# Reordered masking, logarithms and copies in a fused attention and feed-forward kernel, with a third buffer of exponentials

## The reference, cut to what matters

```python
qkv = x @ w_qkv.T; q, k, v = split_heads(qkv); k_y = split_heads(x @ w_ky.T)
L, L_y = q @ k.T / 4, q @ k_y.T / 4
agg = sum(exp(clip(L_y, -15, 15)) * mask, keys) + 1e-6
r = log(abs(L) + 1e-6) - log(agg + 1e-6)
w = softplus(r) * mask
attn = ((w / (sum(w) + 1e-6)) @ v) @ w_proj.T
x = layernorm(x + attn)
h = silu(x @ w1.T * s1) * (x @ w2.T * s2)
h = gelu(h @ h1.T * s_h1); h = gelu(h @ h2.T * s_h2)     # 1024 wide
out = layernorm(x + h @ w3.T * s3)
```

## Time and profile before

| | us |
|---|---|
| median of 3 runs | 1240.26 |
| the profiled execution's own time | 1239.5 |
| its span | 1237.8 |
| PE busy | 1184.8 (96%) |
| DVE busy | 714.9 (58%) |
| ACT busy | 659.0 (53%) |
| POOL busy | 205.5 (17%) |
| first matmul of the feed-forward | at 561.79 |

### The profile page before, as it was taken

One profiled execution on the slowest core, in us unless ns is written; L12 is line 12 of the kernel. 1 busy time (PEld: TensorE's weight loads), 2 busy tenths in 40 slices (PEclk: granted clock), 3 DMA queues, 4 the chain that ended last, 5 costly groups with the idle time before them and its releaser, 6 DMA issues.

```text
span 1237.8 us, 23984 instructions
## 1 busy us (share of the span) xinstructions
PE 1184.8 (96%) x8222; PEld 805.6 (65%) x8222; DVE 714.9 (58%) x1178; ACT 659.0 (53%) x1004; POOL 205.5 (17%) x238
## 2 busy tenths in 40 slices
PE   6899999999999999879999999999999999999997
PEld 2444444544444444437888888888888888888886
DVE  3577778787878787875345435344344353443444
ACT  4688989899888888755114133232242332322421
POOL 2434333434333333300000000000000000000000
PEclk7999999999999999989999999999999999999999
DMA  5555758576776765277000100001000001000010
GB/s 150 120 141 136 215 158 223 156 228 166 216 191 186 204 169 144 56 234 268 34 34 1 36 16 17 34 0 34 17 0 34 17 17 34 0 34 17 0 34 18
DMA packets 62544, 117.28 MB, mean 95 GB/s; under 512 B 8992, under 2 KB 14624, under 8 KB 62496
## 3 DMA queue, kind: packets, MB, share of 16 engines
q1 hardware_dynamic: 62064, 116.12, 32.9%
q10 hardware_dynamic: 432, 0.52, 0.2%
HBM read 46.35 MB, written 19.92 MB: 54 GB/s over the span
## 4 chain that ended last, share of the span: by engine, by line
PE 80%; DVE 9%; issue 5%; ACT 4%; DMA 1%; DVEq 0%; POOL 0%; ACTq 0%; POOLq 0%; SPq 0%
PE score_banks L1360 53%; PE acc_bank L1272 8%; PE score_banks L1244 6%; DVE w_ring L904 4%; PE misc_bank L1236 3%; PE misc_bank L1199 3%; PE misc_bank L1340 2%; ACT w_ring L656 2%; ACT e_ring L649 1%; PE misc_bank L1303 1%; DVE base_v L957 1%; DVE e_ring L895 1%; PE misc_bank L1207 1%; PE misc_bank L1319 1%; DVE e_ring L889 1%
## 5 line engine op out<-in xcount | busy, mean ns | idle before, releaser
L728 ACT ACTIVATE f_h_full<-score_banks,f_scales 128x512 f32<-128x512 f32 x128 | 87.5, 689 | 340.8 <-PE score_banks L1360 340.7
L904 DVE TENSOR_TENSOR w_ring<-score_banks,keep 128x1024 int32<-128x1024 int32 (+1 forms) x192 | 194.0, 1040 | 28.1 <-PE score_banks L1244 27.3
L1360 PE MATMUL score_banks<-f_ha_hi,f_w_all 128*128 128x512 f32 x512 | 204.0, 399 | 0.0
L1360 PE MATMUL score_banks<-f_hb_hi,f_w_all 128*128 128x512 f32 x512 | 203.6, 398 | 0.0
L1360 PE MATMUL score_banks<-f_hb_lo,f_w_all 128*128 128x512 f32 x512 | 201.6, 394 | 0.0
L1360 PE MATMUL score_banks<-f_ha_lo,f_w_all 128*128 128x512 f32 x512 | 200.8, 392 | 0.0
L656 ACT ACTIVATE w_ring<-w_ring 128x1024 f32<-128x1024 f32 (+1 forms) x192 | 172.5, 918 | 24.3 <-DVE w_ring L904 24.2
L649 ACT ACTIVATE e_ring<-score_banks 128x1024 f32<-128x1024 f32 (+1 forms) x192 | 158.3, 877 | 39.4 <-PE score_banks L1244 36.0
L513 POOL TENSOR_SCALAR_AFFINE_SELECT e_ring<-e_ring 128x512 f32<-128x512 f32 (+1 forms) x96 | 80.4, 837 | 285.8 <-DVE e_ring L895 145.0
L1082 DVE CAST f_ha_hi<-f_h_full 128x512 fp32r<-128x512 f32 x64 | 27.3, 426 | 160.5 <-ACT f_h_full L728 160.5
L1360 PEld LDWEIGHTS score_banks<-f_ha_hi,f_w_all 128*128 128x128 f32 x512 | 96.1, 188 | 24.6
(11 more groups left out here) (143 smaller groups left out, 1759.1 us busy)
## 6 DMA issues: line engine op xcount, KB each, us to landing
piece<-in_wf SPq DMA_DIRECT2D x44, 256.0 KB, 2.9
wf_copy<-piece SPq DMA_DIRECT2D x44, 256.0 KB, 3.0
ky_stack<-ky_hi SPq DMA_DIRECT2D x64, 128.0 KB, 2.4
ky_stack<-ky_lo SPq DMA_DIRECT2D x64, 128.0 KB, 2.4
k_stack<-k_hi SPq DMA_DIRECT2D x64, 128.0 KB, 2.6
k_stack<-k_lo SPq DMA_DIRECT2D x64, 128.0 KB, 2.6
f_w_all<-wf_copy SPq DMA_DIRECT2D x2, 4096.0 KB, 24.6
f_x_turn<-x SPq DMA_DIRECT2D x9, 512.0 KB, 3.2
```

Of the source, the lines that this page charges most:

```text
L728: nc.scalar.activation(h_full[m % 2][:], f_bank[m % F_RING], ACT.Gelu, scale=scales[:, 1 + layer, m:m + 1]).then_inc(gelu_done, 1)
L904: nc.vector.tensor_tensor(w_ring[:, t % RING, 2 * i:2 * i + 2, 0:cols].bitcast(I32), pair_banks(place(t, i), cols).bitcast(I32), keep[:, a ...
L1360: mm = nc.tensor.matmul(out, left.bitcast(dt), right.bitcast(dt), start=first and n == 0, stop=last and n == 1)
```

## The change

Nine things are changed, all in the order of the work or in a buffer count:

1. `FIRST_PAIR`: in beats 1 and 2 of a slot DVE does `absolute` of pair 0, then the clip, then `absolute` of pair 1. Before it did the clip first.
2. The check piece of the fifth beat (t = 4) goes to the sixth (t = 5), to a place behind the copies there. `add_differences` goes from the end of beat 1 on DVE to its start, ahead of `keep_agg`.
3. The second `turn` of a finished batch (t = 3) goes behind `sum_weights` on PE, and `turn_keep` behind `copy_sums` on ACT.
4. `E_RING` is 3 (the zone for it is 10 KB larger).
5. `STACK_WARM`: five matmuls of 2x512 on ones, whose result nobody reads, ahead of the first scores.
6. In `beginning`, `scores_y(k, 3)` stands ahead of `ky_proj`, and `scores_y(k, 4)` ahead of `q_proj`.
7. `ending` has a new order on PE, ACT and DVE.
8. The last `sum_weights` of the ending goes into the feed-forward, behind its first tile (m = 0), and `project_out(6, 1)` behind the second. Its `residual` follows on DVE after the third.
9. `residual(6, 0)` goes behind `f_turn_lo` on DVE.

The diff, cut to its core (the ending's lists are shown as rows below):

```diff
-E_RING = 2
+E_RING = 3
+STACK_WARM = 5
-CHECK_BEATS = (0, 2, 3, 4)
+CHECK_BEATS = (0, 2, 3, 5)
+FIRST_PAIR = (1, 2)
...  scalar, slot
-                    if check_step(t, check) is not None:
+                    if t < 5 and check_step(t, check) is not None:
                         check_piece(k, check_step(t, check))
...
+                    if t == 5 and check_step(t, check) is not None:
+                        check_piece(k, check_step(t, check))
-                    if t in (2, 3) and output is not None:
-                        turn_keep(output, t - 2)
+                    if t == 2 and output is not None:
+                        turn_keep(output, 0)
                     if t == 4:
                         k_keep(k)
...
                     if t == CHUNKS:
                         copy_sums(k, 0, (True, 0 in w))
+                    if t == 3 and output is not None:
+                        turn_keep(output, 1)
...  vector, slot
+                    if t == 1 and check_step(0, check) is not None:
+                        add_differences(k.index - FIRST_CHECK - 1)
                     if t == 1 and before[0]:
                         keep_agg(k.shift(-1), 1)
                         factors(k.shift(-1))
...
+                    elif t in w and t in FIRST_PAIR:
+                        absolute(k, t, (0,))
+                        clip(k, t)
+                        absolute(k, t, (1,))
...
-                    if t == 1 and check_step(0, check) is not None:
-                        add_differences(k.index - FIRST_CHECK - 1)
...  tensor, attention_tail and slot
+                if (layer, m) == ("gated", 0):
+                    sum_weights(Unit(BATCH, 1), 2, True)
+                if (layer, m) == ("gated", 1):
+                    project_out(BATCH - 2, 1)
...
                     if sums[1]:
                         sum_weights(*last, not sums[0])
+                    if t == 3 and output is not None:
+                        turn(output, 1)
...  tensor, beginning
+                scores_y(k, 3, y_pair_alone, 1)
                 ky_proj(k1)
-                scores_y(k, 3, y_pair_alone, 1)
                 sum_exps(k, 1, True)
+                scores_y(k, 4, y_pair_alone, 1)
                 q_proj(k1)
                 sum_exps(k, 2, True)
-                scores_y(k, 4, y_pair_alone, 1)
...  tensor, before the run
+            for _ in range(STACK_WARM):
+                nc.tensor.matmul(score[0:2, 2 * BANK_PAIRS - 1, :], ones[:], acc_copy[:], start=True, stop=True)
```

## The result

The changed kernel takes 1244.99 us (median of 18 runs, 1237.76 to 1249.8) against 1239.86 for the kernel before (18 runs, 1237.6 to 1243.02). The ratio is 1.0043, with a 95% interval of 1.0029 to 1.0056: it is slower by 0.43%. The forecast was 1238.6 us, a gain of 0.9 us and too small to tell. So its direction was wrong. The measured time lies just inside the stated range, by 0.01 us at its upper end. The profiled execution took 1243.9 us, with a span of 1242.2 (before: 1239.5 and 1237.8).

The account below looks back on a forecast made before the run. PE bounds the feed-forward from 562 us on; before that it loses little in the loop, more at both attention ends. Terms 0.5 + 0.6 + 0.9 - 1.1 = 0.9 us gained from 1239.5: 1238.6 us, 8-in-10 range 1233.0 to 1245.0.

Parts of the forecast that it names:

- The second turn: Loop, six even slots: the turn's 0.69 us wait mostly moves ahead of the flip; 0.5 us gained, bounds 0 and 4.1.
- Rival A: Loop: the turn's 0.69 us stay won, as the flip needs only `copy_sums` early; 1234.0 us, chance 0.24.
- First pairs ahead of the clip: Loop, beats 1 and 2: beat 3's scores wait less, but the mask comes later; 0.6 us gained in all.
- Rival C: Loop: with the later mask, POOL and DVE collide and beat 3's scores wait; 4 to 5 us, 1243, chance 0.08.
- The check: Loop: its 0.8 us of ACT moves from beat 4 to beat 5, where ACT stands idle; counted as nothing.
- The third buffer: Loop: exponentials wait for scores behind the sums anyway, so two or three buffers are the same; counted as nothing.
- The beginning: First slot: warming and third buffer win 2.9 us, the new order takes most back; 0.9 us gained.
- at full clock: Beginning: after the warming matmuls the first scores start at 17.98 at full clock, taking 0.74 us instead of 1.23.
- Rival D: Beginning: the clock falls again between the first scores, leaving only the third buffer; 1239.2 us, chance 0.55 together with the forecast.
- The ending: End of the attention: new order gains 0.3 us, a low clock on half the chain costs 1.4; 1.1 us lost.
- the flip waits 0.85 us for `copy_sums`: Ending: behind the next beat's scores, the first flip on PE waits 0.85 us for that copy on ACT.
- Rival B: Ending: gaps around the turns drop the clock to 1.2 GHz over all of the chain; 1245.6 us, chance 0.13.

Follow-up runs that it names:

- experiments 1: The changed kernel with the whole ending of before, the two pieces back out of the feed-forward: 1237.87 us, ratio 0.9978 to the kernel before.
- experiment 9: The changed kernel with the ending of before, PE's old order in the first slot and no warming matmuls: 1235.54 us, ratio 0.9963.
- Experiment 4: The changed kernel with PE's old order in the first slot, the warming and the third buffer kept: 1240.65 us, ratio 1.0003.
- experiment 11: The changed kernel with one idle matmul in the 2.0 us wait ahead of the ending's first flip: 1239.59 us, ratio 0.9991.
- Experiments 3: The changed kernel with the readout of the check moved back on DVE, behind the third pair of absolute values: 1242.0 us, ratio 1.0017.

## Why the prediction was wrong

It failed at the ending, in two steps, and at the beginning in one. By its own steps:

*The second turn: forecast 0.5 us, measured 1.4* (0.23 in each of six even slots). The mechanism was right: the gap goes from ahead of the turn to ahead of the flip, with `att_t` as its releaser. Only its size was off, 0.40 in place of 0.6. I had let the second copy start 0.6 us behind the first (349.29 and about 349.9), a whole copy later. In the new trace, one directly behind the other, they start 0.48 apart (347.81 and 348.29). Rival A is out: the flip waits for `att_t` in all six even slots.

*First pairs ahead of the clip: forecast 0.6.* The mask, the stretched cast and the sum that waits for POOL (0.36, forecast 0.44) came as foretold. Taken out alone the edit is worth 0.08 a batch, where the forecast had 0.11 less 0.1 in the loop. Rival C is out: the scores of beat 3 wait for DVE no more, and no sum of an odd slot waits for POOL.

*The check: forecast nothing.* ScalarE's part is worth nothing, as I had said. But the edit has a DVE part, `add_differences`, which I had counted only as something that the clip stands behind. It stood on the path: moving it takes 0.32 us off the wait for beat 3's scores. With the first pairs it is 0.35 a batch (0.58 less the turn's 0.23), and the loop's wins are 3.7 us in the trace in place of 1.1. A batch took 65.12, within the 65.0 to 66.3 that I had set as bounds.

*The third buffer: forecast nothing in the loop, measured 0.01 a batch.* Right.

*The beginning: forecast 0.9 gained.* Against an otherwise equal kernel with the old start (experiments 1 and 9, 1237.87 and 1235.54) it loses 2.3, which their intervals don't tell from nothing. Experiment 4 is clearer: the old order alone, with the warming kept, wins 4.3. The step that failed is "at full clock": I let the warming hold through the first slot, but the clock was low from 22.1 us on, at the second gap of 1.21 us, so the sum, the scores of beat 3 and the projection of ky ran at 1.2 GHz, and the fourth exponentials, behind the copy of ky on ACT, came 2.6 us late. The chain that I followed, in which the projection of q waits for half of the fourth exponentials, was right. It came 2.7 us later than I had it, and for a low clock I had still counted 0.3 gained. Rival D named the reason (the clock falls again in the gaps between the first scores), but I priced it at 0.6 above the forecast.

*The ending: forecast 1.1 lost, measured 7.5 in the trace, 7.1 and 6.8 in the medians.* It splits in two, by experiment 11, which is the new ending with the clock up from 541 us on:

| | forecast | measured |
|---|---|---|
| new order with the clock up (measured: from 541 us on), first flip to feed-forward | 30.6 | 558.13 - 525.81 = 32.3 |
| so against 33.3 before, less the 2.4 put off | 0.3 gained | 1.5 lost |
| low clock on top | 1.4 lost | 38.4 - 32.3 = 6.1 lost |
| together | 1.1 lost | 7.5 lost |

The line for the order holds more of the clock than it says, for both traces have the low stretch near 530 us. Its three groups take 4.3 us there from the first one's start, and some 2.8 at full clock (starts 0.96, 0.84 and 0.99 apart in the trace before), and the scores, the masking and the readout behind them all come later by it. That is an estimate of 1.5 us. By it the order itself would be right (30.8 for 30.6), and the low clock would cost 7.6 us where I had 1.4.

The first failed step is "the flip waits 0.85 us for `copy_sums`". It waited 2.02, for the readout of the check. I had followed DVE's list for what PE's scores need, and had not asked who is the last reader of `misc`. Of the four waits that I had behind it, three came as I had them (1.63, 1.20 and 0.80 us for 1.7, 1.35 and 0.9), and the one of 1.3 us ahead of the scores didn't. The second is the size of the low stretch. I reasoned that the new gaps add up to nearly the old ones, and took half of the chain. What counts isn't their sum. In experiment 11 all gaps behind the flip stand, and the clock stays up; without the matmul ahead of the flip it falls.

Rival B is what happened in effect: 1245.6 by its sum, 1244.99 measured, and a low stretch over most of the chain. That the two times lie so close is luck in part: the ending lost what B had, but the loop won 2.6 us more than B's sum had, the beginning took 1.1 of that back, and the median lies 1.1 above the profiled execution. Nor is B right in its mechanism. It named the gaps behind the turns. Experiments 3 and 11 put the cause ahead of them, in a wait that no rival had. Its test (under 0.6 for more than 10 us) was met: the clock is 0.64 over the 22 us, with a short return, and 0.54 over the 10.7 us from 550.8 to 561.5.

The feed-forward's start at 564.06 lay outside 559 to 562, so my own sign for the ending failed at once. That two pieces were "only put off" was right: they make no gain. In the old ending, with its clock up from 541 us on (experiment 9), the way from the first flip to the feed-forward takes 557.78 - 527.02 = 30.8 us with both pieces in it, against 32.3 + 2.4 for the new one. So the new list is 3.9 us worse with the clock up from 541 us on. Some 1.5 of these can be its low stretch near 530 us; experiment 9 has one there too, but in front of a wait that takes it up (below).

Not settled: how much of the start's low stretches is the edit and how much the run. The second and third slots had one in some traces of like kernels and not in others. Nor is it shown what brings the low stretch near 530 us: all five traces with the new ending have one (0.83 to 0.87 from 526 to 536 us), but so do experiments 1 and 9 with the old one. And that a wait ahead of the flip sets the clock behind it rests on experiments 3 and 11, one trace each beside their medians.

## What to carry to other kernels

When the order around a shared bank changes, write down for each taker who its last reader is and what now stands ahead of that reader on its engine; a side job such as a checksum's readout can be it. Where a trace shows PE's clock falling, price a gap by what the clock takes from all that follows, not by its own length, and try one idle matmul in it before you move the real work. And when single edits taken out don't add up to the whole, look for two that relieve the same wait.

## What the runs showed that was not expected

- One idle matmul of about 1 us in a wait of 2.02 us gained 5.4 us in the median. It didn't have to fill the others: gaps of 1.63, 1.20, 0.87 and 0.56 us stayed in that ending, and the granted clock was 1.00 over them.
- The spread of one kernel's runs goes with its clock. The changed kernel's 18 runs go from 1249.8 us at a mean granted clock of 0.980 to 1237.76 at 0.995. With the wait filled, twelve runs span 1237.79 to 1243.06 at 0.988 to 0.995. A median that moves by some us can be a change in how often a low stretch is met.
- A low stretch can be nearly free. In experiment 9 the clock was 0.83 from 526 to 536 us, and PE's wait for `v_sum` behind it shrank from 2.38 to 0.80 us.
- A copy of 128x512 directly behind another on ACT starts 0.48 us after it, though one alone shows 0.58. The trace before had this too (starts at 32.25 and 32.74 us), and the prediction could have used it.
